# A chunk's values come back from memory on ScalarE's queue instead of SyncE's

## The chip, the core and the metric

The kernel runs on one NeuronCore of a Trainium2 chip. The metric is the device time of one execution in microseconds (us), lower is better. Five engines run instruction streams of their own: TensorE (PE: matmuls, with PEld for their weight loads), VectorE (DVE), ScalarE (ACT), GpSimd (POOL) and SyncE (SP). They wait for each other through semaphores. SyncE begins all transfers between memory and on-chip SBUF in this kernel; the transfers themselves are moved by 16 DMA engines. A DMA-issuing instruction has a duration of its own in the trace (how long the issuing engine stands at it), and a later landing.

## The reference

64 images of 3x224x224 are cut into 196 patches of 16x16, each patch normalised, projected to 256 and normalised again; 77 text tokens are appended, which gives 273 tokens of 256 numbers. Then come an attention block and a channel-mixing block, each with a residual. The attention is unusual, and it explains the transfers that this case is about:

```python
Q, K, V = proj(Wq, bq), proj(Wk, bk), proj(Wv, bv)   # (n, 16 heads, 273 tokens, 16)
scores = jnp.einsum('nqhd,nkhd->nhqk', Q, K) * scale   # 'q','k' run over the heads
attn = jax.nn.softmax(scores, axis=-1)
out = jnp.einsum('nhql,nlhd->nqhd', attn, V)
out = out.reshape(n, s, e)                             # (n, 16, 273, 16) read as (n, 273, 256)
```

So each token attends over its own 16 heads: a 16x16 score matrix per token. To multiply these on TensorE, 16 numbers of a token that lie in a row must come to lie on 16 partitions. The kernel does this by a trip through memory.

## The kernel before, in words

Four images (a quad, 1092 tokens) are three chunks of 364 tokens; there are 16 quads and 48 chunks. A chunk passes through layer norm, the QKV projection (`qkv`, three token tiles of two halves), the attention, the output projection (`wo`), a second layer norm and the mixing block (`k`, `r`, `val`). Matmuls use a high and a low part of each operand.

The attention of a chunk goes like this, with the names of the code:

- `qkv_out` (L508): SyncE writes the three tiles of `qkvt` to `qkv_dram`, one transfer each.
- `qk_in` (L514): one transfer reads queries and keys back into `qk`, 128x48 runs of 32 numbers.
- `v_in` (L524): eight transfers read the values back into `arena`, each 16x48 runs of 16 numbers.
- `kspread` (L921, ScalarE, four operations) copies the keys from `qk` to `arena`; `qplace` (L829, VectorE, two operations) copies the queries to `qx`.
- `s` (L1075, TensorE): the scores, two parts of 48 small matmuls, wait for all of `kspread` and `qplace`.
- `mx`, `sub` (VectorE), `exp` (L926, ScalarE), `pt` (TensorE), `ptc` (L933, ScalarE): softmax without its division, and a transpose.
- `av` (L1096, TensorE): the products with the values. The first part waits for all eight `v_in` transfers of the chunk.
- `rec`, `osb` (L754, L758, VectorE): division. `o_out` (L529): SyncE writes the result in nine transfers; `o_in` (L539) reads it back in four, in the reference's scrambled order; `ont`, `onh`, `wo` go on from there.

Three other streams share SyncE: images to `xim` (`load`, L477), text and patch rows to `hc` (L490, L501), and the results (L546).

The order is written by hand. Table `AT` gives every kind of work a place on a time line that repeats every 4000 units per chunk (3000 per image); `STEPS` holds all places in order; each engine walks through `STEPS` and emits what is due. Every engine's program is therefore a fixed list, run in order: when its next instruction waits, all behind it waits. `v_in` has place 16977, `kspread` 17070 and later, and on ScalarE nothing lies between them.

A transfer adds 16 to its semaphore when it has landed. `qkv_out.wait` holds until a chunk's three tiles are in memory, `av_pe.wait` until the products of the chunk before no longer need the values. `settle` increments a semaphore that nobody waits for, between two waits.

Of the kernel before, what the change touches and what calls it, by code (L numbers as in the profile page):

```python
# [25 lines left out]
HEADS, HD = 16, 16  # L26
IPQ, CPQ = 4, 3
# [7 lines left out]
QKV = 3 * HD  # L35
# [10 lines left out]
PARTS = 2  # L46
# [34 lines left out]
def due(q, step, kind, j):  # L81

    k, rest = divmod(step - AT[kind][j], PERIOD[kind])
    if rest == 0 and exists(q, k, COUNT[kind]):
        yield k


def exists(q, k, count):
    return not isinstance(q, int) or 0 <= count * q + k < count * QUADS
# [97 lines left out]
def fusion_kernel(nc, x, txt, ln1_g, ln1_b, tok_w, tok_b, ln2_g, ln2_b, wq, bq, wk, bk, wv, bv, wo, bo,  # L187
                  w_r, w_k, w_v, mu_r, mu_k, out):
    with ExitStack() as ctx:  # L189
        def sb(name, shape, dt=F32):  # L190
            return ctx.enter_context(nc.sbuf_tensor(name, shape, dt))

        def sig(name, per, primed=False, unit=1):
            return Signal(ctx, nc, name, per, CPQ, primed, unit)
# [24 lines left out]
        y = sb("y", [PT, 2, E])  # L219
# [22 lines left out]
        vb = vrow[:, :, 0:4 * HD].rearrange("p g (y d) -> p g y d", y=4)  # L242
# [19 lines left out]
        r = sb("r", [TT, TILES, E])  # L262
# [6 lines left out]
        qkv_dram = nc.dram_tensor("qkv_dram", (CPQ, CTP, HEADS, QKV), F32, kind="Internal").ap()  # L269
# [7 lines left out]
        prep_pool = ctx.enter_context(nc.semaphore("prep_pool"))  # L277
# [5 lines left out]
        def settle(eng):  # L283
            eng.sem_inc(settled, 1)
# [33 lines left out]
        qkv_out = Own(ctx, nc, "qkv_out", [TILES] * CPQ, 16)  # L318
        qk_in = sig("qk_in", 1, True, unit=16)
        v_in = sig("v_in", 8, True, unit=16)  # L320
# [9 lines left out]
        av_pe = sig("av_pe", PARTS, True)  # L330
# [40 lines left out]
                    r=(r_tanh, [1, 2, 3]), val=(rv_sb, [1, 2, 3]))  # L371
# [7 lines left out]
        def place(kind, j):  # L379
            return banks[BANK[kind][j]]  # L380
# [3 lines left out]
        def square_parts(n, k):  # L384

            src = banks[SPARE[n % len(SPARE)]][:, E * k:E * k + E]
            if n >= 3:
                return (src,) + tuple(wmat[("woT", "wrT", "wkfT", "wvfT")[n - 3]][:, a, k, :] for a in range(2))
            src = src.rearrange("p (h d) -> p d h", d=HD) if n < 2 else src.rearrange("p (h d) -> p h d", d=HD)
            return (src,) + tuple(wqkv[:, a, k, :].rearrange("p (i c) -> p i c", c=QKV)[:, :, HD * n:HD * n + HD] for a in range(2))  # L390
# [16 lines left out]
        def weights_due(q, s):  # L407
            return [n for n, v in enumerate(WEIGHTS_AT) if v == QUAD * q + s]
# [22 lines left out]
        POOL_ALL = 30  # L431
# [4 lines left out]
        def _(sp):  # L436
# [25 lines left out]
            def after(signal, q, k, steps):  # L462
                signal.wait(sp, q, k, steps)
                settle(sp)

            def after_all(own, q, k):
                own.wait(sp, q, k)
                settle(sp)

            def body(q):  # L470
                for s in STEPS:
                    for k in due(q, s, "load", 0):
                        if q * IPQ + k > 0:
                            after(x_stats, q, k - 1, 1)
                        src = x[bass.ds(q * IPQ + k, 1), :, :, :].rearrange("b c (i r) w -> (b c i) (r w)", r=PS)
# [33 lines left out]
                    for k in due(q, s, "qk_in", 0):  # L509
# [2 lines left out]
                        after(q_sb, q, k - 1, 2)  # L512
                        src = qkv_dram[k % CPQ, :, :, 0:2 * HD]
                        qk_in.done(sp.dma_start(qk[:, :, :], src.rearrange("(g t) i j -> (t i) g j", t=8)))  # L514
                    for k in due(q, s, "v_in", 0):
                        if q * CPQ + k == 0:
                            sp.wait_ge(prep_pool, POOL_ALL)
                        after_all(qkv_out, q, k)
                        after(av_pe, q, k - 1, PARTS)
                        src = qkv_dram[k % CPQ, :, :, 2 * HD:QKV].rearrange("(r g y) i j -> r y i g j", r=2, y=4)  # L520
                        for rr in range(2):
                            for yy in range(4):
                                p = 64 * rr + HEADS * yy
                                v_in.done(sp.dma_start(vb[p:p + HEADS, :, yy, 0:HD], src[rr, yy]))  # L524
                    for k in due(q, s, "o_out", 0):
                        after(o_sb, q, k, PARTS)
                        after(on_in, q, k - 2, ROW_DMAS)
# [3 lines left out]
                    for k in due(q, s, "o_in", 0):  # L531
# [5 lines left out]
                        for m, r0, rows, i, p in row_pieces(k % CPQ):  # L537
                            src = o_dram[m, :, :, :].rearrange("q t d -> (q t d)").rearrange("(r e) -> r e", e=E)
                            on_in.done(sp.dma_start(on[p:p + rows, i, :], src[r0:r0 + rows, :]))  # L539
                    for i, (o, rows) in enumerate(TOK):  # L540
                        for k in due(q, s, "out", i):
# [4 lines left out]
                            out_dma.done(sp.dma_start(dst[bass.ds(q * (IPQ * T) + (CT * k + o), rows), :], h2[0:rows, k % CPQ, i, :]))  # L546

            quads(sp, body)
            out_dma.wait(sp, QUADS - 1, CPQ - 1, 3)
            qk_in.wait(sp, QUADS - 1, CPQ - 1, 1)  # L550
# [333 lines left out]
        def _(act):  # L884
# [3 lines left out]
            def prep(ins):  # L888
                ins.then_inc(prep_act, 1)
                count[0] += 1  # L890
                return count[0]
# [8 lines left out]
            def square_weight(n):  # L900
                act.wait_ge(prep_pe, 3 + n)
                for k in range(2):
                    src, hi, lo = square_parts(n, k)
                    c = prep(A.activation(hi, src, ACT.Copy, scale=SCALE.get(n, 1.0)))
                if n == len(WEIGHTS) - 1:
                    act.wait_ge(raw_in, RAWS * 16)
                    for x in range(3):
                        src = bnat[:, x, :].rearrange("p (h d) -> p d h", d=HD) if x < 2 else bnat[:, x, :].rearrange("p (h d) -> p h d", d=HD)
                        c = prep(A.activation(bqkv[:, :, HD * x:HD * x + HD], src, ACT.Copy, scale=SCALE[0] if x == 0 else 1.0))
                    assert c == ACT_ALL  # L910

            def body(q):
                for s in STEPS:
                    for n in weights_due(q, s):
                        square_weight(n)
                    for yy in range(4):
                        for k in due(q, s, "kspread", yy):
                            if yy == 0:
                                qk_in.wait(act, q, k, 1)
                                s_pe.wait(act, q, k - 1, PARTS)  # L920
                            kb_sb.done(A.activation(kb[:, :, yy, :], qk[:, :, HD:2 * HD], ACT.Copy, scale=ymask[:, yy:yy + 1]))  # L921
# [15 lines left out]
                    for job, (w0, w1) in enumerate(XCUT):  # L937
# [8 lines left out]
                        for k in due(q, s, "xh", job):  # L946
# [3 lines left out]
                            src = place("x", job)[:, 0:XROWS * (w1 - w0)].rearrange("p (w j) -> p j w", j=XROWS)  # L950
# [59 lines left out]
                    for i, (o, rows) in enumerate(TOK):  # L1010
                        for k in due(q, s, "rt", i):
                            r_pe.wait(act, q, k, i + 1)
                            out_sb.wait(act, q, k - 1, 3)
                            r_tanh.done(A.activation(r[0:rows, i, :], place("r", i)[0:rows, 0:E], ACT.Tanh, scale=0.5))

            quads(act, body)

        @block.tensor
# [190 lines left out]
```

## Time and profile before

| what | value |
|---|---|
| median of 3 runs | 1631.94 us (1626.0 to 1637.81) |
| profiled execution: span from first to last instruction | 1635.7 us |
| TensorE's mean granted clock in it | 0.968 of full speed |
| PE, DVE, ACT, POOL busy | 89%, 81%, 67%, 60% |
| transfers by hardware queue | 702394 packets, 224.23 MB, 77.9% of 16 DMA engines' time |

The profiled execution is one of its own beside the three timed ones; the page gives its span, and its whole time is not listed apart from the runs. Its span lies 3.8 us (0.2%) above their median. The whole pipeline repeats 48 times, so that 1 us per chunk is 48 us of the kernel, or 3%. Busy shares count the work of an engine alone: waits, and instructions that only begin a transfer, do not count, so SyncE has no busy share at all.

### The profile page before, as it was taken

The page shows a single profiled execution, that of the slowest core. Times are in us where ns is not written, and L with a number is a line of the kernel's source. Part 1 is how long each engine was busy: PE and PEld are TensorE (multiplying, and loading weights), DVE is VectorE, ACT ScalarE, POOL GpSimd, SP SyncE. Part 2 cuts the span into 40 slices and gives each one's busy share as a digit, 9 for nine tenths or more (in the row PEclk, how much of TensorE's full clock was granted, in tenths as well). Part 3 has the DMA queues.
Part 4 walks back from the last instruction along what each step waited for, and adds up shares of the span by engine and source line. Part 5 has one row for each costly group of instructions (what it writes and reads, how often), then busy time and mean ns, then how long its engine had stood idle before and what let it go on. Part 6 is the DMA issues. An engine that isn't in the chain of part 4 may idle for free. (4 is left out here: it accounts for less than half of the span.)

```text
span 1635.7 us, 53680 instructions
## 1 busy us (share of the span) xinstructions
PE 1454.6 (89%) x18762; PEld 1382.2 (85%) x18762; DVE 1332.3 (81%) x3075; ACT 1099.9 (67%) x2230; POOL 973.6 (60%) x1507
## 2 busy tenths in 40 slices
PE   4678899899999999999999999999999999998856
PEld 4677898898998898889898898998988988897756
DVE  5576888798988989898898888898898988888642
ACT  4455777677777776776777676777777776775543
POOL 2121566567656666666766765675675676576556
PEclk8798999999999999999999999999999999999988
DMA  4279979889877887888887896898898799887651
GB/s 121 59 141 138 141 147 150 125 159 157 143 157 141 147 155 143 150 137 165 149 140 157 151 141 127 167 157 141 152 154 140 151 159 140 156 151 118 131 74 37
DMA packets 702658, 227.65 MB, mean 139 GB/s; under 512 B 617470, under 2 KB 673854, under 8 KB 702394
## 3 DMA queue, kind: packets, MB, share of 16 engines
q1 hardware_dynamic: 702394, 224.23, 77.9%
q8 instruction: 153, 2.51, 0.8%
q14 instruction: 111, 0.91, 0.2%
HBM read 121.64 MB, written 89.64 MB: 129 GB/s over the span
## 5 line engine op out<-in xcount | busy, mean ns | idle before, releaser
L1026 PE MATMUL bank<-wqkv,xnT 128*126 128x384 f32 (+1 forms) x1728 | 354.2, 349 | 5.5 <-issue 5.5
L1118 PE MATMUL bank<-wtok,xT 128*98 128x258 f32 x2304 | 310.2, 290 | 12.0 <-DVE xT L770 11.4
L1026 PEld LDWEIGHTS bank<-wqkv,xnT 128*126 128x126 f32 (+1 forms) x1728 | 294.0, 185 | 18.3 <-issue 10.2
L1118 PEld LDWEIGHTS bank<-wtok,xT 128*98 128x98 f32 x2304 | 294.2, 171 | 14.6 <-DVE xT L770 13.2
L667 POOL TENSOR_TENSOR mixp<-mixf,mixp 128x364 fp32r<-128x364 f32 x192 | 185.2, 976 | 107.2 <-ACT mixp L1000 106.6
L921 ACT ACTIVATE arena<-qk,ymask 128x768 f32<-128x768 f32 x192 | 164.0, 926 | 97.6 <-DMA qk<-qkv_dram 97.6
L843 DVE TENSOR_TENSOR qkvt<-bank,bqkv 126x384 f32<-126x384 f32 (+1 forms) x288 | 154.0, 548 | 48.5 <-PE bank L1026 47.0
L654 POOL TENSOR_TENSOR dT<-zT 128x364 f32<-128x364 f32 x96 | 79.7, 851 | 153.9 <-ACT zT L994 153.9
L609 POOL TENSOR_TENSOR rs<-ve,small 126x3 f32<-126x3 f32 (+1 forms) x160 | 150.3, 940 | 12.5
L607 POOL TENSOR_TENSOR ve<-mv,small 126x3 f32<-126x3 f32 (+1 forms) x160 | 58.8, 368 | 158.8 <-DVE mv L865 104.0
L765 DVE TENSOR_REDUCE xs<-xim 84x14 f32<-84x1792 f32 x64 | 128.7, 2011 | 23.1 <-ACT xim L955 22.8
L872 DVE SCALAR_TENSOR_TENSOR mixf<-dT,mus,zT 128x364 f32<-128x364 f32 x192 | 125.8, 676 | 22.4 <-POOL zT L661 19.5
L943 ACT ACTIVATE xcols<-xim 84x640 f32<-84x640 f32 (+1 forms) x192 | 126.1, 693 | 25.4 <-DMA xim<-in_x 24.1
L1026 PE MATMUL bank<-woT,onT 128*126 128x256 f32 (+1 forms) x864 | 121.9, 287 | 12.4 <-DVE onT L849 12.1
L951 ACT ACTIVATE xT<-bank 128x420 fp32r<-128x420 f32 (+1 forms) x192 | 99.9, 532 | 44.5 <-PE bank L1106 44.2
L1026 PE MATMUL bank<-wrT,mixp 128*126 128x256 f32 (+1 forms) x864 | 124.9, 292 | 4.2 <-POOL mixp L667 3.7
L1026 PEld LDWEIGHTS bank<-woT,onT 128*126 128x126 f32 (+1 forms) x864 | 110.6, 186 | 17.7 <-DVE onT L849 16.9
L1026 PE MATMUL bank<-mixp,wkfT 128*128 128x364 f32 x576 | 123.5, 352 | 1.5 <-POOL mixp L667 1.4
L1075 PE MATMUL bank<-arena,qx 128*32 128x64 f32 x4608 | 83.0, 225 | 43.8 <-issue 43.8
L933 ACT ACTIVATE pt<-bank 64x384 f32<-64x384 f32 x192 | 93.0, 484 | 37.9 <-PE bank L1083 34.5
L682 POOL TENSOR_TENSOR h<-h,r 126x256 f32<-126x256 f32 x144 | 114.2, 807 | 6.1 <-DVE r L878 6.1
L1075 PEld LDWEIGHTS bank<-arena,qx 128*32 128x32 f32 x4608 | 74.1, 112 | 51.1 <-issue 47.4
(121 smaller groups left out, 3339.6 us busy)
## 6 DMA issues: line engine op xcount, KB each, us to landing
xim<-in_x SPq DMA_DIRECT2D x128, 294.0 KB
qk<-qkv_dram SPq DMA_DIRECT2D x48, 768.0 KB, 8.3
qkv_dram<-qkvt SPq DMA_DIRECT2D x96, 378.0 KB
arena<-qkv_dram SPq DMA_DIRECT2D x384, 48.0 KB, 3.9
qkv_dram<-qkvt SPq DMA_DIRECT2D x48, 336.0 KB
o_dram<-probs SPq DMA_DIRECT2D x288, 48.0 KB, 1.9
out<-h SPq DMA_DIRECT2D x96, 126.0 KB
on<-o_dram SPq DMA_DIRECT2D x64, 126.0 KB
```

Source lines behind the costliest of these rows:

```text
L609: done.done(P.tensor_tensor(rs[:, :], ve[:, :], powt[0:part, 0:ve.shape[1]], ALU.pow))
L667: mix_lo.done(P.tensor_tensor(mixp[:, w, 1, kk, :], mixf[:, kk, :], mixp[:, w, 0, kk, :].bitcast(F32), ALU.subtract))
L682: out_sb.done(P.tensor_tensor(dst, dst, r[0:rows, i, :], ALU.add))
L765: x_stats.done(V.tensor_reduce(xs[:, :], xim[:, :].rearrange("p (w q) -> p w q", q=128), AX.X, ALU.add))
L843: qkv_sb.done(V.tensor_tensor(qkvt[0:rows, i, NQ * half:NQ * half + NQ], place("qkv", job)[0:rows, 0:NQ], bqkv[0:rows, :, :].rearrange("p ...
L872: mix_sb.done(V.scalar_tensor_tensor(out=mixf[:, kk, :], in0=dT[:, kk, :], scalar=mus[:, w, kk:kk + 1], in1=zT[:, kk, 0:CT], op0=ALU.mult, ...
L921: kb_sb.done(A.activation(kb[:, :, yy, :], qk[:, :, HD:2 * HD], ACT.Copy, scale=ymask[:, yy:yy + 1]))
L943: x_cols.done(A.activation(xcols[:, 128 * w0:128 * w1].rearrange("p (w r q) -> p w r q", r=HALF, q=PS), xim[:, :].rearrange("p (r w q) -> ...
L951: x_hi.done(A.activation(xT[:, 0, :, w0:w1], src, ACT.Copy))
L1026: ins = mm(psum, left(a, k), right(b, k), start=t == 0, stop=t == len(terms) - 1)
L1075: ins = mm(place("s", part)[32 * j:32 * j + 32, col:col + 64], qx[:, g, :, :].rearrange("p x q -> p (x q)"), kb[:, g, :, :].rearrange("p y ...
L1118: ins = mm(place("tok", c)[0:PT, 0:E + 2], xT[:, a, i0:i0 + GRID // 2, :].rearrange("p i w -> p (i w)"), wtok[:, b, ch, :], start=t == 0, ...
```

## The change

The block that begins the eight `v_in` transfers is taken out of SyncE's program and put in ScalarE's, at the same place of `STEPS`, with the same three waits and the same `settle`. There it stands right ahead of `kspread`. The transfers themselves, their source, destination, size and semaphore stay as they are.

```diff
--- SyncE, body(q)
-                    for k in due(q, s, "v_in", 0):
-                        if q * CPQ + k == 0:
-                            sp.wait_ge(prep_pool, POOL_ALL)
-                        after_all(qkv_out, q, k)
-                        after(av_pe, q, k - 1, PARTS)
-                        src = qkv_dram[k % CPQ, :, :, 2 * HD:QKV].rearrange("(r g y) i j -> r y i g j", r=2, y=4)
-                        for rr in range(2):
-                            for yy in range(4):
-                                p = 64 * rr + HEADS * yy
-                                v_in.done(sp.dma_start(vb[p:p + HEADS, :, yy, 0:HD], src[rr, yy]))
--- ScalarE, body(q), right ahead of "kspread"
+                    for k in due(q, s, "v_in", 0):
+                        if q * CPQ + k == 0:
+                            act.wait_ge(prep_pool, POOL_ALL)
+                        qkv_out.wait(act, q, k)
+                        settle(act)
+                        av_pe.wait(act, q, k - 1, PARTS)
+                        src = qkv_dram[k % CPQ, :, :, 2 * HD:QKV].rearrange("(r g y) i j -> r y i g j", r=2, y=4)
+                        for rr in range(2):
+                            for yy in range(4):
+                                p = 64 * rr + HEADS * yy
+                                v_in.done(act.dma_start(vb[p:p + HEADS, :, yy, 0:HD], src[rr, yy]))
```

The eight instructions move from one list to another. On ScalarE, at one chunk, the program reads before (`dT` at L1005 is the rectified product of the mixing block, `arena<-qk,ymask` is `kspread`):

```order
437 L977 ACTIVATE onT<-bank 128x364 x2
438 L1000 ACTIVATE mixp<-mixf 128x364
439 L1005 ACTIVATE dT<-bank 128x364 x2
440 L921 ACTIVATE arena<-qk,ymask 128x48x16 x4
441 L960 ACTIVATE mean<-bank 98x1
```

and with the change, at the same chunk (its lines are one further down, and L916 is the moved transfer):

```order
451 L978 ACTIVATE onT<-bank 128x364 x2
452 L1001 ACTIVATE mixp<-mixf 128x364
453 L1006 ACTIVATE dT<-bank 128x364 x2
454 L916 DMA arena<-qkv_dram 16x48x16 x8
455 L922 ACTIVATE arena<-qk,ymask 128x48x16 x4
```

Eight issues now stand between the rectified product and `kspread`; nothing else moved.

On SyncE, from one chunk's `qk_in` on, the program reads before:

```order
62 L514 DMA qk<-qkv_dram 128x48x32
63 L490 DMA hc<-in_txt 56x256
64 L490 DMA hc<-in_txt 21x256
65 L524 DMA arena<-qkv_dram 16x48x16 x8
66 L477 DMA xim<-in_x 42x1792 x2
67 L508 DMA qkv_dram<-qkvt 126x768
```

and with the change:

```order
61 L514 DMA qk<-qkv_dram 128x48x32
62 L490 DMA hc<-in_txt 56x256
63 L490 DMA hc<-in_txt 21x256
64 L477 DMA xim<-in_x 42x1792 x2
65 L508 DMA qkv_dram<-qkvt 126x768
```

The image's load and the write of the next chunk's first tile now follow the text rows at once; what stands ahead of `qk_in` is the same.

## Rows read from the trace of the kernel before

**Rows 1.** The page: span, engines' busy us (share), hardware DMA queue.

```profile
span 1635.7 us, 53680 instructions
...
PE 1454.6 (89%) x18762; PEld 1382.2 (85%) x18762; DVE 1332.3 (81%) x3075; ACT 1099.9 (67%) x2230; POOL 973.6 (60%) x1507
...
q1 hardware_dynamic: 702394, 224.23, 77.9%
```

**Rows 2.** Windows, one middle stretch: start:end, length, busy us by engine, clock, DMA.

```profile
core 0: us, PE busy (x) PEld busy (x) DVE busy (x) ACT busy (x) POOL busy (x), PEclk, DMA share, GB/s
200.00:1400.00 1200.00, 1124.01 (x14956) 1072.59 (x14955) 1048.72 (x2420) 862.93 (x1761) 771.53 (x1174) 0.99 0.84 149
```

**Rows 3.** Waits of PE: who <- whom, us in total, times, longest us.

```profile
PE bank L1075 <- issue: 43.8, 35, 4.9
```

**Rows 4.** Waits of ACT.

```profile
ACT arena L921 <- DMA qk<-qkv_dram: 97.6, 46, 4.3
```

**Rows 5.** Waits of SP.

```profile
SPq L284 <- DVE probs L758: 60.3, 37, 10.1
```

**Rows 6.** Timeline, PE, one chunk: start, us, engine, line, operation [idle before <-releaser].

```profile
853.29 1.60 PE L1075 MATMUL bank<-arena,qx 128*32 128x64 f32 x96 [0.59 <-issue]
...
859.91 1.77 PE L1096 MATMUL bank<-arena,pt 128*32 128x68 f32 x96
885.17 1.60 PE L1075 MATMUL bank<-arena,qx 128*32 128x64 f32 x96 [1.61 <-issue]
...
892.12 1.75 PE L1096 MATMUL bank<-arena,pt 128*32 128x68 f32 x96
```

**Rows 7.** Timeline, DVE, the same chunk: division and placing of queries.

```profile
862.09 0.56 DVE L758 TENSOR_TENSOR probs<-bank,mx 128x384 f32<-128x384 f32 x1
...
881.80 1.14 DVE L829 COPY qx<-qk 64x768 f32<-64x768 f32 x2 [0.87 <-DMA qk<-qkv_dram]
```

**Rows 8.** Timeline, SP's transfers, the same chunk: start, us until the last is begun.

```profile
862.82 5.20 SPq L529 DMA_DIRECT2D o_dram<-probs  x9
868.13 0.35 SPq L508 DMA_DIRECT2D qkv_dram<-qkvt  x1
868.74 2.51 SPq L501 DMA_DIRECT2D hc<-yh  x3
871.52 1.46 SPq L539 DMA_DIRECT2D on<-o_dram  x4
873.24 0.39 SPq L514 DMA_DIRECT2D qk<-qkv_dram  x1
873.82 4.92 SPq L490 DMA_DIRECT2D hc<-in_txt  x2
878.92 0.33 SPq L546 DMA_DIRECT2D out<-h  x1
879.44 5.50 SPq L524 DMA_DIRECT2D arena<-qkv_dram  x8
885.05 0.86 SPq L477 DMA_DIRECT2D xim<-in_x  x2
```

**Rows 9.** Timeline, ACT, the same chunk.

```profile
878.63 0.83 ACT L1005 ACTIVATE dT<-bank 128x364 f32<-128x364 f32 x2
881.66 3.41 ACT L921 ACTIVATE arena<-qk,ymask 128x768 f32<-128x768 f32 x4 [2.20 <-DMA qk<-qkv_dram]
...
888.80 0.99 ACT L926 ACTIVATE probs<-probs 128x384 f32<-128x384 f32 x2 [2.48 <-DVE probs L746]
```

**Rows 10.** Line L524 (values): issue ns min/median/max; landing us min/median/max.

```profile
L524 SPq DMA_DIRECT2D arena<-qkv_dram x384: 309/523/3663, 100.9 to 1563.3; - x192
...
DMA to landing us min/median/max: 2.7/3.9/7.0
```

**Rows 11.** Timeline, SP, other chunks: eight values' transfers, fastest and slowest.

```profile
693.95 4.33 SPq L524 DMA_DIRECT2D arena<-qkv_dram  x8
...
904.42 5.00 SPq L477 DMA_DIRECT2D xim<-in_x  x2
...
910.12 8.93 SPq L524 DMA_DIRECT2D arena<-qkv_dram  x8
```

**Rows 12.** Timeline, SP and ACT, two chunks: a plain write-out, and rows to `hc`.

```profile
144.43 4.02 SPq L529 DMA_DIRECT2D o_dram<-probs  x9
...
840.99 9.12 SPq L501 DMA_DIRECT2D hc<-yh  x4
...
847.73 0.47 ACT L1005 ACTIVATE dT<-bank 128x364 f32<-128x364 f32 x1
```

**Rows 13.** Timeline, all engines, a chunk whose scores do not wait for ScalarE.

```profile
818.54 3.42 ACT L921 ACTIVATE arena<-qk,ymask 128x768 f32<-128x768 f32 x4 [2.99 <-DMA qk<-qkv_dram]
...
822.54 1.83 PE L1075 MATMUL bank<-arena,qx 128*32 128x64 f32 x96
```

## The prediction

> **What bounds the kernel now.** I read the page first, then the middle stretch by windows, the waits by engine, and last one chunk in the timeline, engine by engine.
>
> The page shows no engine that is full: TensorE is busy for 1454.6 of 1635.7 us, ScalarE for 1099.9 [rows 1]. In the middle TensorE is busy for 1124 of 1200 us, at a granted clock of 0.99, the level of 2.4 GHz, and ScalarE for 863 [rows 2]. So I looked for a ring of waits that closes once per chunk. The waits give both ends: TensorE stands idle ahead of the scores in 35 of the 48 chunks [rows 3], and ScalarE waits for `qk_in` to land in 46 of 48, 97.6 us in all, 2.03 us per chunk of 48 [rows 4].
>
> One chunk in the timeline closes the ring. Scores begin at 853.29, the value products at 859.91 [rows 6], the division ends at 862.09 + 0.56 = 862.65 [rows 7]. SyncE begins the write-out 0.17 us later, and then has no long pause: the write-out, the last QKV tile, rows to `hc`, the reads of `on`, and `qk_in` at 873.24 [rows 8]. `kspread` starts at 881.66, when `qk_in` lands, and takes 3.41 us, to 885.07; the next scores begin at 885.17 [rows 6, 9]. The queries are placed by 881.80 + 1.14 = 882.94 [rows 7], so it is `kspread` that TensorE waits for. The ring is 6.62 + 2.74 + 0.17 + 10.42 + 8.42 + 3.51 = 31.88 us, which is the whole distance of two chunks' scores. Whoever lengthens a link of it lengthens the kernel, 48 times. `v_in`, in contrast, is issued on SyncE at 879.44, behind `qk_in`, in a stretch that is not in the ring: SyncE later waits idle for the division in 37 chunks [rows 5, 8].
>
> **What the change removes.** SyncE loses eight issues per chunk, 4.3 to 8.9 us of its time [rows 11]. They lie behind `qk_in` and ahead of SyncE's idle wait, so most of this is worth nothing. Two small gains may follow. In the 11 chunks in which SyncE did not wait for the division it was late; I give it 0.5 us each, 5 us. And a write-out of nine takes 5.20 us in the chunk shown and 4.02 in a clean one [rows 8, 12], since earlier transfers are still in the queue. Fewer of them could bring part of that back: I take 0.2 us per chunk, 10 us in all; the bounds are 0 and 1.18 x 48 = 57.
>
> **What the change adds.** ScalarE now begins the eight transfers in the place in which it used to wait for `qk_in`, and `kspread` can only start behind them. The trace has no transfer issued by ScalarE, so the price must be bounded.
> - From below: each at the shortest issue on record, 0.309 us, is 2.5 us for eight [rows 10].
> - Nearest: a whole group of eight on SyncE with little else in the queue, 4.33 us; 17 of the 48 groups take 4.3 to 4.6 [rows 11]. It fits the median of 0.523 us for one [rows 10]. And it looks like a price per piece: 0.523 us for 768 pieces is 0.68 ns each, by which the 6144 pieces of `qk_in` cost 4.2 us, and indeed the instruction behind `qk_in` stands for most of 4.92 us [rows 8], although `qk_in` itself shows 0.39.
> - From above: 5.5 us, as in the chunk shown [rows 8]; 8.93 is behind an image's load in the same queue [rows 11], which ScalarE's own queue would not be.
>
> I take 4.33, the nearest in kind, an empty queue. To it come 0.2 us for the waits and the `settle` ahead of it, as SyncE has between 878.92 + 0.33 and 879.44 [rows 8], and 0.1 until the next operation starts, as TensorE's start behind `kspread` [rows 6, 9]: 4.63 us. The wait of 2.03 us for `qk_in`, which ScalarE had anyway, hides its part. `kspread` starts later by 4.63 - 2.03 = 2.60 us, 125 us over 48 chunks.
>
> The Trainium skill weighs against such a price: DMA: Bandwidth & Descriptors, § Issuing engines are not separate DMA queues, says that issuing from several engines saves only the sequencer's time to initiate a transfer, "which is usually small relative to the DMA itself". By it the hold on ScalarE would be about nothing and the sum about zero. The row disagrees: median issue 0.523 us against a median landing of 3.9, times eight in a row [rows 10]; I go by the row.
>
> **What of it lies on the path.** In 35 chunks all of it, as TensorE already stands there. In the other 13 the scores start a little behind `kspread` for another reason: 818.54 + 3.42 = 821.96 and then 822.54 [rows 13], 0.58 us, of which 0.1 is the usual start. I take 0.8 us of cover for each, 10 us: 125 - 10 = 115. Nothing further on in the ring gives it back, since every link starts at the end of the one before: TensorE goes from scores to value products in 6.6 and 6.95 us of its own work [rows 6], and `exp` waits 2.48 us for VectorE [rows 9], so ScalarE's lateness is taken up there.
>
> Contention: the values' packets now start about 2 us before `qk_in` lands, and can delay that landing; but ScalarE is held until 2.60 us past the old landing anyhow, so up to that much is covered. If this cover is gone, see the third rival. The value products get their data sooner relative to the scores: no cost.
>
> A last credit: ScalarE's queue may run ahead of its arithmetic, and begin the transfers while the last rectified product (about 0.42 us, half of 0.83 [rows 9]) is still running. Bounds 0 and 0.42 x 48 = 20 us below; I take half of it, 10 us, on the unmeasured side.
>
> **Sum.** 115 - 5 - 10 - 10 = +90 us, on the profiled 1635.7 us of span: 1726. The median of the runs is 3.8 us lower, and the forecast is for such a median: 1631.94 + 90 = 1722 us. With a hold of 2.5 us in place of 4.33 the sum is 90 - 88 = +2; with 5.5 it is 90 + 56 = +146, or 1778.
>
> **Rivals.**
> 1. *ScalarE is hardly held* (the price at its lower bound, because an issue on an empty queue of its own is handed over at once). Speaks for it: single issues at 0.309 us. Against: those occur amid long ones, and groups of eight never took under 4.3 us [rows 10, 11]. About +2 us, 1634.
> 2. *Faster: it was the issuing that bound.* SyncE is in the ring from the write-out to `qk_in`, 873.24 - 862.82 = 10.42 us per chunk [rows 8], almost without a pause. If freeing its queue shortens this, and the hold is as in rival 1 and starts under the running operation, the ring gets shorter: write-outs at 4.02 instead of a middle of about 4.6 are 0.6 x 48 = 28 us, the late starts 5, so 1632 - 33 = 1599. The deciding point is a hold of 2.03 us: above it ScalarE gives to the ring more than its wait covers. Against: nothing of `v_in` stands between write-out and `qk_in`. The skill's Perfetto Trace Analysis, § DMA Optimizations, states the rule that would make it so: where an engine is busy with generating descriptors, balance the transfers over the engines that can issue them.
> 3. *Slower by more: the two queues collide.* SyncE's instruction behind `qk_in` stands long, for four transfers to `hc` 9.12 us, until 850.11, while ScalarE is free at 847.73 + 0.47 = 848.20 [rows 12]. If ScalarE's issues must wait for SyncE's, that is 1.9 us more in every third chunk, +30 us (1752, inside the range). If besides the issues run as behind an image, 8.93 us in 16 chunks and 5.5 in 32 [rows 8, 11], the mean is 6.64, and the sum 90 + (6.64 - 4.33) x 48 = +201, 1833. The skill's same page, § DMA Instruction — HWDGE, describes this: the descriptor generator is shared and locked for one instruction's use, and the time of that lock counts in the issue.
>
> **Chances.** Forecast (1685 to 1795, hold of 3.7 to 5.5 us and collisions up to rival 3's first part) 0.73; rival 1 (1625 to 1665) 0.10; rival 2 0.06; rival 3 in full 0.11. The range is 1655 to 1795: it leaves out rival 2, most of 1 and all of full 3. A change below about 1% (16 us) can't be told from none in this kernel. Faster by over 1% is rival 2, 0.06; within 1% is most of rival 1 and a little else, 0.09; slower 0.85.
>
> **What would show it.** In the changed profile: ScalarE's eight issues span about 4.3 us and begin with the end of the rectified product; its wait for `qk_in` ahead of `kspread` is nearly gone; TensorE's idle time ahead of L1075 grows from 43.8 us to about 135; the distance of scores rises by about 2 us; SyncE's wait for the division grows; the distance from division to `qk_in` stays at 10 to 11 us. Wrong is the price if the eight span under 3 us; wrong is the ring if they span 4.3 and the time does not move, because slack elsewhere takes it up; and if `qk_in` lands well over 8.4 us after its issue, it is contention and not the issuing that costs.

## The result: 1959 us, a fifth slower than before

| | median | runs | ratio to before, 95% interval |
|---|---|---|---|
| before | 1633.84 us | 4 (1626.0 to 1637.81) | |
| with the change | 1958.99 us | 4 (1955.53 to 1970.7) | 1.201 [1.197, 1.206] |

The change costs 325 us. The forecast was +90, its range ended at 1795: the direction was right, the size wrong by a factor of 3.6. The profiled execution took 1959.84 us, with a span of 1958.0.

### The profile page after: what moved, and what is told of

The parts are those of the page before. It is cut to its first block and busy times, and to the rows that moved or that the text cites. A ratio compares the mean times of both kernels' runs of the same rounds, so it can differ in the third digit from the quotient of the medians.

```text
span 1958.0 us, 53632 instructions
## 1 busy us (share of the span) xinstructions
PE 1523.5 (78%) x18762; PEld 1452.0 (74%) x18762; DVE 1329.9 (68%) x3075; ACT 1101.4 (56%) x2230; POOL 969.7 (50%) x1507
## 3 DMA queue, kind: packets, MB, share of 16 engines
q10 hardware_dynamic: 301056, 18.90, 13.9%
## 5 line engine op out<-in xcount | busy, mean ns | idle before, releaser
L922 ACT ACTIVATE arena<-qk,ymask 128x768 f32<-128x768 f32 x192 | 163.6, 922 | 383.7 <-issue 383.7
L1027 PE MATMUL bank<-wqkv,xnT 128*126 128x384 f32 (+1 forms) x1728 | 375.5, 364 | 3.6 <-issue 3.6
L1076 PE MATMUL bank<-arena,qx 128*32 128x64 f32 x4608 | 135.0, 313 | 310.8 <-issue 306.5
L1076 PEld LDWEIGHTS bank<-arena,qx 128*32 128x32 f32 x4608 | 124.8, 164 | 319.4 <-issue 319.4
L1027 PEld LDWEIGHTS bank<-wqkv,xnT 128*126 128x126 f32 (+1 forms) x1728 | 313.3, 196 | 19.8 <-issue 15.4
L731 DVE TENSOR_REDUCE mx<-bank 128x24 f32<-128x384 f32 x96 | 53.6, 558 | 239.2 <-PE bank L1076 239.2
L760 DVE TENSOR_TENSOR xT<-bank,xT 128x420 fp32r<-128x420 f32 (+1 forms) x192 | 103.3, 552 | 66.5 <-ACT xT L952 66.3
L611 POOL TENSOR_TENSOR var<-stat,mean 98x2 f32<-98x2 f32 x64 | 16.9, 263 | 260.3 <-issue 146.1
L1027 PE MATMUL bank<-woT,onT 128*126 128x256 f32 (+1 forms) x864 | 121.0, 285 | 14.4 <-DVE onT L839 14.3
```

The source lines that it names most:

```text
L760: x_lo.done(V.tensor_tensor(xT[:, 1, :, w0:w1], src, xT[:, 0, :, w0:w1].bitcast(F32), ALU.subtract))
L1027: ins = mm(psum, left(a, k), right(b, k), start=t == 0, stop=t == len(terms) - 1)
L1076: ins = mm(place("s", part)[32 * j:32 * j + 32, col:col + 64], qx[:, g, :, :].rearrange("p x q -> p (x q)"), kb[:, g, :, :].rearrange("p y ...
```

## The profile after

The page, its header, busy line and hardware queues, beside [rows 1]:

```profile
span 1958.0 us, 53632 instructions
...
PE 1523.5 (78%) x18762; PEld 1452.0 (74%) x18762; DVE 1329.9 (68%) x3075; ACT 1101.4 (56%) x2230; POOL 969.7 (50%) x1507
...
q1 hardware_dynamic: 401338, 205.34, 52.8%
q10 hardware_dynamic: 301056, 18.90, 13.9%
```

ScalarE does the same work (1101 us); it and all others only stand longer. TensorE is busy for 69 us more with the same matmuls, so its clock fell: the mean granted clock is 0.892 instead of 0.968. The values' 301056 packets now have a queue of their own, q10.

Waits in total (who <- whom, us, times, longest), ScalarE, TensorE and SyncE, beside [rows 3 to 5]:

```profile
ACT arena L922 <- issue: 383.7, 48, 11.2
```

```profile
PE bank L1076 <- issue: 306.5, 48, 9.8
```

```profile
SPq L284 <- DVE qkvt L833: 312.0, 81, 13.8
...
SPq L284 <- DVE probs L748: 99.3, 48, 18.5
```

ScalarE's idle time ahead of `kspread` was 97.6 us and is 383.7, or 8.0 us per chunk; its label is "issue", time in which an engine waits for nothing that the profile names; the timeline below shows its own transfers' issues in it. TensorE's ahead of the scores grew from 43.8 to 306.5 us. SyncE waits for the division in all 48 chunks: it has time to spare that nobody needs.

One chunk in the timeline, of the kind shown in [rows 6 to 9] (text rows behind `qk_in`). First SyncE's transfers:

```profile
930.21 0.39 SPq L514 DMA_DIRECT2D qk<-qkv_dram  x1
930.80 5.04 SPq L490 DMA_DIRECT2D hc<-in_txt  x2
936.02 0.33 SPq L536 DMA_DIRECT2D out<-h  x1
```

ScalarE, its work (ACT) and its issues (ACTq) mixed:

```profile
933.23 1.69 ACT L956 ACTIVATE xim<-xcols 84x1792 f32<-84x1792 f32 x1
933.92 0.89 ACTq L916 DMA_DIRECT2D arena<-qkv_dram  x2
934.83 0.49 ACT L1001 ACTIVATE mixp<-mixf 128x364 fp32r<-128x364 f32 x1
934.83 0.55 ACTq L916 DMA_DIRECT2D arena<-qkv_dram  x1
935.22 0.46 ACT L1006 ACTIVATE dT<-bank 128x364 f32<-128x364 f32 x1
935.41 2.18 ACTq L916 DMA_DIRECT2D arena<-qkv_dram  x1
935.57 0.47 ACT L1006 ACTIVATE dT<-bank 128x364 f32<-128x364 f32 x1
937.62 7.20 ACTq L916 DMA_DIRECT2D arena<-qkv_dram  x4
944.92 3.41 ACT L922 ACTIVATE arena<-qk,ymask 128x768 f32<-128x768 f32 x4 [8.88 <-issue]
```

VectorE, which waits for the same landing and shows when it was:

```profile
938.96 1.14 DVE L819 COPY qx<-qk 64x768 f32<-64x768 f32 x2 [1.45 <-DMA qk<-qkv_dram]
```

TensorE, scores and value products:

```profile
948.42 2.81 PE L1076 MATMUL bank<-arena,qx 128*32 128x64 f32 x96 [8.28 <-issue]
...
956.60 1.61 PE L1097 MATMUL bank<-arena,pt 128*32 128x68 f32 x92
```

The reader is to see four things. The issues begin at 933.92, while four earlier operations are unfinished (the one at 933.23 and the three behind it). The first three are quick, 0.3 to 0.55 us. Then they stand: the last five take 2.18 and 7.20 us, and end at 944.82, 6 us after `qk_in` landed. And the scores' 96 matmuls take 2.81 us where they took 1.60 [rows 6].

The ring of the prediction, read in the same way off 44 chunks (the third to the forty-sixth), in us. The last three rows are no links of it.

| mean per chunk | before | after | difference x 48 |
|---|---|---|---|
| scores to value products | 6.75 | 8.04 | +62 |
| value products to division | 2.77 | 2.81 | +2 |
| division to the end of the write-out's nine issues | 4.92 | 4.58 | -16 |
| write-out to `qk_in`'s issue | 4.55 | 4.52 | -1 |
| `qk_in`'s issue to landing | 8.42 | 9.15 | +35 |
| landing to `kspread` | 0.04 | 5.35 | +255 |
| `kspread` | 3.42 | 3.41 | 0 |
| `kspread` to scores | 0.34 | 0.10 | -12 |
| ring | 31.21 | 37.96 | +324 |
| *first of the eight issues, after `qk_in`'s issue* | 7.67 | 5.33 | |
| *last of the eight ends, after `qk_in`'s landing* | 5.06 | 5.24 | |
| *values landed, after `qk_in`'s issue* | 16.96 | 18.02 | |

The ring accounts for the whole loss. The italic rows point at its cause: the issues begin 2.3 us earlier than before, and still end about as far behind `qk_in`'s landing. On SyncE that end held up nobody. On ScalarE it holds up `kspread`.

The equal means, 5.06 and 5.24, are in part chance. There are three kinds of chunks, by what SyncE issues right behind `qk_in`: rows to `hc`, text rows, an image's load. In them the distance goes from 5.80 to 4.38, from 3.55 to 5.25 and from 5.89 to 6.15 us. Within the changed kernel the same three kinds begin the eight 7.2, 4.2 and 4.6 us after `qk_in`'s issue and end them after 14.3, 14.1 and 14.8: an earlier start hardly brings an earlier end.

## The experiments

Means of the ring in the experiments, for reference below:

| us | after | e1 | e2 | e3 | e6 | e7 | e9 |
|---|---|---|---|---|---|---|---|
| eight issues, first to last | 9.07 | 7.06 | 4.39 | 7.46 | 5.32 | 9.13 | 5.64 |
| `qk_in` issue to landing | 9.15 | 8.36 | 8.27 | 8.31 | 8.84 | 8.97 | 6.06 |
| landing to `kspread` | 5.35 | 7.20 | 1.66 | 0.03 | 1.89 | 5.54 | 5.08 |
| scores to value products | 8.04 | 8.27 | 7.29 | 10.24 | 7.43 | 6.46 | 7.46 |
| ring | 37.96 | 39.16 | 32.53 | 34.33 | 33.58 | 36.87 | 33.94 |

### e1: begin only when `qk_in` has landed

```diff
                         av_pe.wait(act, q, k - 1, PARTS)
+                        settle(act)
+                        qk_in.wait(act, q, k, 1)
```

> The changed kernel with one more wait: ScalarE begins the eight values' transfers only once qk_in has landed. Theory A (backlog: the issues end about 5.2 us after qk_in lands however early they start, since the DMA engines must first take in qk_in's pieces and then the values'): the eight issues now span 4.3 to 5.3 us instead of 9.1, kspread starts 4.5 to 5.5 us after the landing as before, the time is 1900 to 1960 us, hardly lower than the changed kernel's 1959. Theory B (an issue by ScalarE costs over 1 us by itself): the span stays 9 us, kspread starts 9 us after the landing, 2130 us. Theory C (the two queues in flight at once slow each other, and that is the loss): kspread starts 4.5 us after the landing and qk_in lands 0.7 us sooner, 1870 to 1890 us.

Measured: 2008.5 us, ratio 1.229 [1.219, 1.238]. `qk_in` lands 0.8 us sooner, as theory C has it, but the issues then take 7.06 us and `kspread` starts 7.20 us behind the landing. So meeting `qk_in` in flight is not the loss: without it the kernel is 49 us slower. A start 3.05 us later (8.38 instead of 5.33 us after `qk_in`'s issue) ends the issues only 1.05 us later. Theory B, a high price of each issue on ScalarE, had 9 us and 2130, too high; theory A had the span too short, for even behind `qk_in`'s landing the DMA engines have other work. In the three kinds of chunks the span is 5.9, 8.9 and 6.4 us. In the longest kind SyncE issues an image's load in the middle of ScalarE's eight, where before it stood behind them; in the last it issues rows to `hc`. Whether these are what lengthens the span was not tested.

### e2 and e5: hardly any pieces, on either engine

e2 is the changed kernel, e5 the kernel before; `act` is `sp` in e5. The call stands inside `v_in.done(...)`, as in the change.

```diff
-   act.dma_start(vb[p:p + HEADS, :, yy, 0:HD], src[rr, yy])
+   act.dma_start(vb[p:p + HEADS, 0:1, yy, 0:HD], src[rr, yy][:, 0:1, :])
```

> The changed kernel, but each of the eight transfers brings 16 pieces instead of 768 (one group of 48; the other 47/48 of the values are left out). Theory A (pieces): the issues take 8 x 0.3 to 0.55 = 2.5 to 4.4 us, end before qk_in lands, kspread starts within 0.1 us of the landing; 1560 to 1640 us. Theory B (a price per issue on ScalarE): span still 8 to 9 us, over 1900 us.

> The kernel before (SyncE begins the values' transfers), each of the eight with 16 pieces instead of 768 (47/48 of the values are left out). With e2 it makes a square: pieces or none, SyncE or ScalarE. Theory A (SyncE's place is off the ring, the pieces' load on the 16 DMA engines is hidden there): 1600 to 1635 us, and the price on ScalarE, without pieces, is 1699 less this, 65 to 100 us. Rival (the values' pieces slow the ring's own transfers already before the change, a good part of the loss would be there in both): under 1580 us.

Measured: e2 1699.3 us, ratio 1.039 [1.034, 1.045]; e5 1616.0 us, ratio 0.989 [0.985, 0.992]. With the two kernels of the case they make a square:

| | SyncE issues | ScalarE issues | the move costs |
|---|---|---|---|
| 16 pieces each | 1616 | 1699 | 83 |
| 768 pieces each | 1634 | 1959 | 325 |
| the pieces cost | 18 | 260 | |

Of 325 us, 83 are the price of eight issues in that place of ScalarE's order, and 242 arise only from the pieces together with that place. Of the 83, 30 stand between scores and value products (7.29 us in e2, 6.67 in e5), at a mean granted clock of 0.949 against 0.971. Theory A had e2's issues right at its upper end, 4.4 us, but not their place: begun 5.39 us after `qk_in`'s issue, they end 1.51 us behind its landing at 8.27. One chunk of e2, ScalarE and then SyncE:

```profile
1171.26 0.31 ACTq L916 DMA_DIRECT2D arena<-qkv_dram  x1
1171.60 0.70 ACTq L916 DMA_DIRECT2D arena<-qkv_dram  x1
1172.33 4.22 ACTq L916 DMA_DIRECT2D arena<-qkv_dram  x6
1176.66 3.41 ACT L922 ACTIVATE arena<-qk,ymask 128x768 f32<-128x768 f32 x4 [4.36 <-issue]
```

```profile
1163.54 0.39 SPq L514 DMA_DIRECT2D qk<-qkv_dram  x1
```

Transfers of 16 pieces, and still about half a microsecond each: a group takes 4.39 us on the mean (4.10 in e5), about the same as the clean groups of 768 pieces on SyncE in [rows 11]. The median of one issue is 0.442 us in e2 and 0.420 in e5, against 0.523 for 768 pieces [rows 10].

### e6: half the pieces

```diff
-   act.dma_start(vb[p:p + HEADS, :, yy, 0:HD], src[rr, yy])
+   act.dma_start(vb[p:p + HEADS, 0:24, yy, 0:HD], src[rr, yy][:, 0:24, :])
```

> The changed kernel with half of each transfer, 384 pieces instead of 768 (half of the values are left out). Theory A (beyond a floor of 0.55 us per issue, ScalarE is held by the pieces' backlog): between e2's 1699 and the changed kernel's 1959, near the middle, 1790 to 1860 us; kspread starts 3 to 4 us after qk_in lands. Rival (a threshold: the loss comes once a queue is full): under 1740 us.

Measured: 1751.5 us, ratio 1.071 [1.055, 1.088], between the two expectations; `kspread` starts 1.89 us behind the landing, not 3 to 4. The first half of the pieces costs 52 us, the second 207. This fits a larger of two: the floor of 4.4 us, under which half the pieces nearly fit (5.32), and the time until the DMA engines have begun most of the pieces (9.07). The values land 14.15 us after `qk_in`'s issue with half the pieces and 18.02 with all: 3.87 us for 3072 pieces, 1.26 ns each. That is a price of these pieces alone: e9, below, takes 6016 pieces out of `qk_in` and brings the values' landing from 18.02 to 15.32 us, 0.45 ns each.

### e9: `qk_in` with few pieces, as many bytes

```diff
-   src = qkv_dram[k % CPQ, :, :, 0:2 * HD]
-   qk_in.done(sp.dma_start(qk[:, :, :], src.rearrange("(g t) i j -> (t i) g j", t=8)))
+   src = qkv_dram[k % CPQ, :, :, :].rearrange("(p x) i j -> p (x i j)", p=128)
+   qk_in.done(sp.dma_start(qk[:, :, :].rearrange("p g j -> p (g j)"), src[:, 0:2 * HD * GR]))
```

> The changed kernel, but qk_in reads the same 768 KB as 128 runs of 6 KB instead of 6144 runs of 128 bytes (they hold other numbers than queries and keys, so the attention is another one). Theory A (the values' issues stand because the DMA engines must first take qk_in's many pieces; pieces and not bytes): the eight issues by ScalarE span 4.4 to 5.5 us instead of 9.1, at the same distance behind qk_in's issue, and kspread starts 9.5 to 11 us after it instead of 14.5; 1690 to 1790 us. Rival (bytes count): span over 8 us, over 1900 us.

Measured: 1767.1 us, ratio 1.081 [1.075, 1.088]. The eight issues of the unchanged 768 pieces now span 5.64 us instead of 9.07, and `kspread` starts 6.06 + 5.08 = 11.1 us behind `qk_in`'s issue instead of 14.5. Time and direction are theory A's, the two spans 0.1 us past its limits; `qk_in`'s bytes are excluded. Of the 4.7 us by which the span was beyond the floor, 3.4 go with the pieces of another transfer, on another engine's queue. It shares with them the 16 DMA engines.

Those pieces alone hold nobody on ScalarE, though. In e2 they are all there, and the issues run at the floor. The packet records of the changed kernel's trace join the two. Each transfer puts 784 packets in ScalarE's queue (301056 / 384: 768 pieces and 16 more). No issue ends with more than 2583 of that queue's packets not yet begun, and the last of the eight ends, on the mean, with 1656. While `qk_in` is in flight, 398 of them begin per us, and 610 behind its landing. So ScalarE fills its own queue with the first transfers, and then stands until the DMA engines have begun enough of it, which `qk_in`'s pieces slow: the first issue of over 0.7 us is the second, third or fourth of the eight, in 6, 12 and 26 of 44 chunks. That the queue has a limit is read from these counts and was not tested; it is no single count, as issues of over 0.7 us end mostly with 1100 to 2200. Nor is all of the slowing explained: behind the landing it is 662 per us in e1 and 927 in e9, although `qk_in` is done in both.

### e3: behind `kspread`

The block of the change is moved inside `kspread`'s loop, after its fourth operation:

```diff
                             kb_sb.done(A.activation(kb[:, :, yy, :], ...))
+                            if yy == 3:
+                                ... # the same waits and the eight act.dma_start
```

> The eight transfers stay with ScalarE but stand right behind the four operations of kspread. Theory A: kspread starts at qk_in's landing again, the issues behind it span about 4.3 us (nothing of qk_in is left), exp and the value products are late by 2 to 4 us instead of the scores by 5.4; 1700 to 1800 us. Rival (the hold costs the same wherever it stands in ScalarE's order): 1900 to 1960 us.

Measured: 1773.1 us, ratio 1.085 [1.079, 1.090], in theory A's range. 186 us of the 325 are gone, the scores start as before, and the price moves on: scores to value products is 10.24 us instead of 6.75. One chunk of ScalarE:

```profile
1162.52 0.94 ACT L911 ACTIVATE arena<-qk,ymask 128x768 f32<-128x768 f32 x1 [1.56 <-DMA qk<-qkv_dram]
1162.61 0.94 ACTq L922 DMA_DIRECT2D arena<-qkv_dram  x2
...
1167.84 4.48 ACTq L922 DMA_DIRECT2D arena<-qkv_dram  x4
1172.42 0.17 ACT L961 ACTIVATE mean<-bank 98x1 f32<-98x1 f32 x1 [6.49 <-issue]
```

The issues begin with the first of the four operations, and `kspread` is out of their way; the 6.49 us of idle time come behind it, ahead of `exp`. Their span is 7.46 us, not the 4.3 expected, though `qk_in` has landed; e1 has the same (7.06).

### e4 and e7: keep TensorE busy in the wait

```diff
+   for _ in range(WARM):      # e4: 40, all ahead of the waits
+       mm(place("s", part)[:, 0:128], ident[:, :], ident[:, :], start=True, stop=True)
    q_sb.wait(pe, q, k, 2)
    kb_sb.wait(pe, q, k, 4)
```

In both, `turn(...)`, the wait for the bank, moves ahead of them. e7 has 20, the second ten behind `q_sb` and the first of `kspread`'s four operations.

> The changed kernel with 40 unneeded 128x128 matmuls into the scores' bank while TensorE waits ahead of the scores. Theory A (scores to value products grew from 6.75 to 8.04 us because TensorE's granted clock falls in the wait): the distance returns to 6.7 to 7.0 us, the time falls by 45 to 65 us to 1895 to 1915. Rival (that distance grew because ScalarE is behind with its other work ahead of exp): 8.0 us stays, time 1955 or more.

> The changed kernel with 20 unneeded 128x128 matmuls of about 0.22 us ahead of the scores, ten when the bank is free and ten when the first of kspread's four operations is done, so that they end before the scores could start (e4's 40 ran 2.4 us past that). If the low granted clock is what lengthens scores to value products: 6.4 to 7.0 us there instead of 8.04, scores start within 0.3 us of kspread's end, time 1880 to 1910. Rival (no gain beyond what is spent): 1950 or more.

Measured: e4 1992.9 us, ratio 1.219 [1.211, 1.227]; e7 1913.9 us, ratio 1.171 [1.154, 1.188]. The distance falls to 6.38 and 6.46 us, from 8.04, so the clock is shown as the cause of that growth, and the rival excluded. In e4 the 40 ran 2.4 us beyond `kspread`'s end on the mean and ate the gain: the time is beyond both expectations. In e7 the scores start 0.62 us behind `kspread`, not 0.3, and the time misses the expected 1910 by 4 us. e7's line of the scores' matmuls (count, ns min/median/max), then the same of the changed kernel and of the kernel before:

```profile
L1081 PE MATMUL bank<-arena,qx x4608: 219/219/316, 106.7 to 1840.5; 128*32 128x64 f32 x192
```

```profile
L1076 PE MATMUL bank<-arena,qx x4608: 216/314/316, 109.2 to 1890.1; 128*32 128x64 f32 x192
```

```profile
L1075 PE MATMUL bank<-arena,qx x4608: 216/219/316, 104.6 to 1567.9; 128*32 128x64 f32 x192
```

### e8, e10, e11: what else the ring allows

SyncE's 4.55 us between write-out and `qk_in` are the link that an order of issues can shorten. e8 gives the four reads of `on` to ScalarE, with their waits. e10 and e11 leave all on SyncE and change two places of the table:

```diff
--- e8, on the kernel before: the block "o_in" moves to ScalarE, ahead of "kspread"
+   on_in.done(act.dma_start(on[p:p + rows, i, :], src[r0:r0 + rows, :]))
--- e10
-   qk_in=[15678], ... o_in=[23572]
+   qk_in=[14945], ... o_in=[22940]
--- e11
+   qk_in=[15015], ... o_in=[23010]
```

> The kernel before, values on SyncE as they were, but ScalarE begins the four reads of the attention's output (o_in), which have few pieces (364 rows of 1 KB). SyncE has them in the ring, 1.5 us ahead of qk_in. Theory A (a price of 0.3 to 0.5 us per issue on ScalarE, not in its tight place, and 1.5 us less in the ring): 1570 to 1625 us. Rival (ScalarE, waiting in its order for the write-out to land, is held at a place where TensorE or GpSimd needs it): 1660 or more.

> The kernel before, values on SyncE, with two places of the table changed: o_in 23572 to 22940 and qk_in 15678 to 14945, so that both follow the last QKV tile at once, ahead of the image's load, the rows to hc and the text rows. Theory A (the ring's link from the last write-out's issue to qk_in falls from 4.55 us to 3.5 to 3.9, nothing else in the ring grows): 1585 to 1615 us. Rival (the rows to hc and the text, now behind qk_in's backlog, come late for the layer norm): 1630 or more.

> The kernel before, values on SyncE, o_in at place 23010 and qk_in at 15015: as e10, but the image's load stays ahead of both (e10's third of the chunks with that load grew to 39.0 us of ring, with ScalarE waiting for the image, while another third fell to 29.0). In that third the order is as before, in the two others the rows to hc, or the text rows, go behind qk_in. Theory A (a shorter ring is time gained if nothing else is late): ring 31.3, 29.0 to 29.6 and 30.5 to 31.5 us, time 1585 to 1625 us. Rival (the rows to hc, late by qk_in's backlog of 5 us, hold the next layer norm): 1640 or more.

Measured: e8 1680.8 us, 1.028 [1.010, 1.046]; e10 1735.0 us, 1.061 [1.057, 1.066]; e11 1618.0 us, 0.9895 [0.9854, 0.9936]. e8 gains 1.1 us in the link aimed at and loses more elsewhere: ScalarE is free 0.5 us behind `qk_in`'s landing where it was 1.9 ahead of it, and TensorE waits 77.3 us for ScalarE's normalised rows (`xn`) where it waited 11. That is the rival's time and its effect; whether the wait for the write-out or the four issues hold ScalarE there was not separated. Its two runs lie 1% apart, so the size is rough. e10's time is also the rival's, but it is the image's load that comes late, behind `qk_in`; ScalarE's waits show it, against 24.1 us before:

```profile
ACT xcols L943 <- DMA xim<-in_x: 166.0, 38, 10.4
```

e11 leaves that load ahead and is faster than both kernels of the case, by 1.05% against the one before: little, but all its six runs (1613 to 1623 us) lie under all eleven of the kernel before beside it (1627 to 1648). Its SyncE, a chunk in which the rows to `hc` go behind:

```profile
857.35 0.35 SPq L508 DMA_DIRECT2D qkv_dram<-qkvt  x1
857.95 1.46 SPq L539 DMA_DIRECT2D on<-o_dram  x4
860.32 0.39 SPq L514 DMA_DIRECT2D qk<-qkv_dram  x1
860.95 5.83 SPq L501 DMA_DIRECT2D hc<-yh  x3
```

`qk_in` follows the last tile after 2.97 us; in the same kind of chunk before it was 5.11 [rows 8]. Its three rings are 31.0, 29.4 and 32.0 us: the last grew from 31.0, not the 30.5 to 31.5 expected, and takes back part of the gain.

## Why the prediction was wrong

**The ring was right.** All 325 us stand in it, and nothing outside gave any of them back. That SyncE's freed time is worth almost nothing was right too: 16 us in the write-out, where 15 were counted, and term by term: 7 from its earlier start (5 forecast) and 9 from shorter issues (10 forecast). The cover ahead of the scores, counted as 10 us, was 12.

**The step that failed is the hold on ScalarE**, "I take 4.33, the nearest in kind, an empty queue". With the waits and the start it was 4.63 us, and the measured idle time ahead of `kspread` is 8.0 (383.7 / 48). From landing to `kspread` the change adds 255 us where the sum had 125; of the 235 us by which the forecast was short, 130 are here. Two things were wrong in it. The price was read as a duration that starts when ScalarE starts. It is more of an end: in the changed kernel the eight end 14.1 to 14.8 us after `qk_in`'s issue, whether they begin after 4.2 or 7.2. The trace of before gave a sign of it: in its chunk they end at 879.44 + 5.50 = 884.94, 3.3 us behind `qk_in`'s landing [rows 8, 9], and on the mean 5.06 behind it. And an empty queue of its own did not make ScalarE's issues cheap: the long groups, 8.93 us behind an image [rows 11], were set aside for that reason, while the values' own pieces fill that queue, by the counts under e9, and e9 shows that pieces on the other queue keep it full for longer.

**The reason given for 4.33 failed as well.** "0.68 ns each" for a piece came from 0.523 us for 768, but transfers of 16 pieces take nearly the same half microsecond in a row of eight (e2, e5). It is a floor per transfer; the pieces count once the queue is full. The floor alone gives about what the forecast said: e2 is 65 us above the kernel before and 83 above e5, and 90 were forecast.

**Two terms were missing.** TensorE's clock, 62 us in the ring: at 0.99 in the middle [rows 2] it was taken for granted, and the text worked out no price for 8 us of waiting. And `qk_in`'s landing, 0.73 us later, 35 us. It was called covered up to 2.60 us, but the hold ended 5.35 us behind the later landing, so nothing was covered. With half of the values' pieces it is 8.84 (e6), with hardly any 8.27 (e2), so the 0.73 come from them. The prediction's sign for contention, a landing well over 8.4 us, thus showed (9.15), yet e1, which puts it back to 8.36, is slower still.

**The credit was harmless.** ScalarE's queue does run ahead, by more than the 0.42 us allowed: 1.2 us on the mean, with two to four operations unfinished. It helps next to nothing, as the end hardly depends on the start.

**Rivals.** The third, two queues that collide, was nearest, and its 0.11 too little; but 1833 was still low, and its mechanism is another. The Trainium skill's Perfetto Trace Analysis, § DMA Instruction — HWDGE, has a generator locked for one instruction; in the chunk shown the first of SyncE's two text transfers stands for 4.66 us, from 930.80 to 935.46, and three of ScalarE's issues go through inside that stretch at 0.3 to 0.55 us. A lock held for the whole of SyncE's instruction isn't seen there. The same section of the Trainium skill also knows a descriptor buffer that can be too small for what is generated. It does not say that an issue stands for it; the three quick issues and the standing behind them would fit. The first rival, by the rule that issuing saves only a small time, falls with e2: even without pieces it is 83 us. The second, to balance transfers over engines, fails twice, here and in e8: other engines wait for what ScalarE has to do next at those places.

## What to carry to other kernels

An engine that issues several transfers of many small pieces fills its own queue, and then stands until the DMA engines have begun most of the pieces (e2, e6, e9 and the packet counts); transfers of other queues in flight make that longer. So price a moved group of issues by when it ends relative to the transfers in flight, not by its shortest duration. Before moving them to a compute engine, look at what stands right behind them in its order, and whether the old engine's delay ever held anyone. And where TensorE would come to wait for several microseconds each round, add the price of its matmuls at the lower clock.

## What was not expected of the hardware

- ScalarE's issues are handed over while up to four earlier operations are unfinished: 933.92 against 935.57 + 0.47 = 936.04 for the end of the last.
- A row of eight transfers costs about half a microsecond each on either engine, with 16 pieces (4.39 us on ScalarE, 4.10 on SyncE) as with 768 in a clean group (4.33 on SyncE).
- In 26 of 44 chunks ScalarE hands over three transfers of 768 pieces within 0.7 us each, even while 6144 pieces of SyncE's are in flight. The fourth stands longer in 38 of 44, and no issue ends with more than 2583 of its queue's packets not begun.
- With idle stretches of 6 us ahead of the scores (306.5 / 48), the same matmuls take 314 ns at the median where they took 219, and the mean granted clock falls to 0.892; the two levels are 1.2 and 2.4 GHz. Twenty unneeded matmuls in the wait (e7) bring the median back to 219 ns, the mean granted clock to 0.962, and 45 us.
